# Two heads' attention scores on the two row halves of TensorE, in a two-layer adaLN transformer kernel

## The reference

```
qkv = x @ Wqkv
q = qkv[..., :512]    -> 32 query heads of 16      k, v -> 8 heads of 16
k = repeat(k, 4)                                    v = repeat(v, 2)
scores = q @ k^T / sqrt(16), causal over 2048 keys
aw = softmax(scores)
aw = aw[:, :, 0] - lam * aw[:, :, 1]                (pairs of heads)
attn = (aw @ v) * (1 - LAMBDA_INIT)
y = attn @ Wproj, then transposed, reshaped and @ Wproj again
```

## Time and profile before

| | |
|---|---|
| median of 3 runs | 2494.93 us (2493.49 to 2496.83) |
| span of the profiled execution | 2499.5 us |
| layer 0 attention, first to last pass | about 122 to 2013 us of the span |
| PE / DVE / ACT / POOL busy | 90% / 73% / 64% / 21% |
| granted TensorE clock, mean | 0.941 |

### The profile page before, as it was taken

How to read it: one execution, slowest core, us unless ns; L and a number is a source line. 1 busy time by engine, 2 the same in 40 slices (tenths; PEclk the granted TensorE clock), 3 DMA queues, 4 the chain that set the end, 5 groups by cost and what they waited for, 6 DMA issues and landing times. The chain is left out here.

```text
span 2499.5 us, 46449 instructions
## 1 busy us (share of the span) xinstructions
PE 2245.5 (90%) x13164; PEld 950.5 (38%) x13164; DVE 1826.9 (73%) x4038; ACT 1595.2 (64%) x3105; POOL 517.9 (21%) x573
## 2 busy tenths in 40 slices
PE   6799989999999999989998999899999869889984
PEld 4133323332333333333333333333333248657841
DVE  3888877877787787878787888788888528534467
ACT  2177767776777677767776767677777735335633
POOL 1113021221212121212121212121301014200067
PEclk8599999999999999999999999999999979899955
DMA  5210211112020202020202020202010030000001
GB/s 151 39 28 20 45 30 35 36 28 40 25 40 25 40 25 39 29 36 28 58 6 59 6 58 7 58 8 56 14 22 1 1 94 0 0 1 1 1 17 50
DMA packets 92964, 78.79 MB, mean 32 GB/s; under 512 B 47008, under 2 KB 79904, under 8 KB 92704
## 3 DMA queue, kind: packets, MB, share of 16 engines
q1 hardware_dynamic: 92704, 75.61, 13.3%
HBM read 26.81 MB, written 16.78 MB: 17 GB/s over the span
## 5 line engine op out<-in xcount | busy, mean ns | idle before, releaser
L726 ACT ACTIVATE probs<-b_bank 128x512 f32<-128x512 f32 (+1 forms) x2304 | 1224.1, 575 | 466.6 <-PE b_bank L883 438.1
L583 DVE TENSOR_REDUCE m_part<-a_bank 128x2 f32<-128x1024 f32 x768 | 917.2, 1221 | 202.7 <-PE a_bank L874 200.4
L883 PE MATMUL b_bank<-q_pack,k_pack 98*128 98x512 bf16 (+3 forms) x2560 | 798.9, 356 | 53.4 <-issue 26.0
L874 PE MATMUL a_bank<-k_pack,q_pack 96*128 96x512 bf16 (+3 forms) x2560 | 688.0, 358 | 67.5 <-DVE m_part L579 31.5
L901 PE MATMUL acc<-probs,v_tile 128*32 128x512 f32 (+3 forms) x5120 | 588.7, 541 | 14.6 <-ACT o_sb L733 14.1
L579 DVE CUSTOM_DVE_ANT_0 a_bank<-a_bank,mask_a 128x128 f32<-128x128 f32 (+3 forms) x1024 | 478.1, 518 | 145.2 <-PE a_bank L874 137.0
L883 PEld LDWEIGHTS b_bank<-q_pack,k_pack 98*128 98x128 bf16 x2560 | 240.2, 98 | 679.3 <-ACT probs L726 338.3
L449 POOL TENSOR_SCALAR_AFFINE_SELECT probs<-probs 128x512 f32<-128x512 f32 (+1 forms) x192 | 151.5, 789 | 1090.9 <-ACT probs L726 1090.9
L874 PEld LDWEIGHTS a_bank<-k_pack,q_pack 96*128 96x128 bf16 x2560 | 222.2, 99 | 314.8 <-DVE m_part L583 91.8
L901 PEld LDWEIGHTS acc<-probs,v_tile 128*32 128x32 f32 x5120 | 107.4, 108 | 242.6 <-issue 116.7
L579 DVE DVE_READ_ACCUMULATOR2_ANT m_part<- 128x1 f32 x1024 | 145.3, 142 | 0.1
(11 more groups left out here) (188 smaller groups left out, 1709.5 us busy)
## 6 DMA issues: line engine op xcount, KB each, us to landing
q_pack<-part SPq DMA_DIRECT2D x384, 64.0 KB, 2.4
scratch<-qkv_row SPq DMA_DIRECT2D x16, 512.0 KB, 2.8
heads<-scratch SPq DMA_DIRECT2D x16, 512.0 KB, 3.6
k_pack<-part SPq DMA_DIRECT2D x96, 64.0 KB, 2.3
xg<-in_L_attn_x SPq DMA_DIRECT2D x16, 256.0 KB, 2.8
scratch<-qkv_row SPq DMA_DIRECT2D x32, 128.0 KB, 2.7
q_pack<-m_rows SPq DMA_DIRECT2D x256, 2.0 KB
x<-in_L_attn_x SPq DMA_DIRECT2D x4, 1024.0 KB, 12.0
```

Of the source, the lines that this page charges most:

```text
L583: dve.tensor_reduce(m_part[:, 2 * hp:2 * hp + 2, t, c], bank[:, :, 0:w], AX.X, ALU.max).then_inc(a_maxed, A_INC)
L726: act.activation(probs[:, s % P_RING, h, at:C], b_bank[bank_no(("B", par, s, h))][:, at:C], ACT.Exp, scale=HD ** -0.5) \
L874: ins = pe.matmul(a_bank[unit % A_RING][:, k, 0:w], q_pack[buf][0:KP_ROWS, 2 * hp + k, q:q + P], k_pack[buf][0:KP_ROWS, C * c:C * c + w], ...
L883: ins = pe.matmul(b_bank[bank_no(("B", par, s, h))][:, at:at + C - q], k_pack[par][0:KP_ALL, P * kt:P * (kt + 1)], q_pack[par][0:KP_ALL, h ...
```

## The change

- q and k parts are packed again, in two slices of at most 64 rows: the first slice holds four pieces (64 rows), the second two pieces and the two maxima rows (34 rows). Even heads sit in partitions 0 to 63, odd heads in 64 to 127, and `k_pack` is there twice. A score tile of a step is now two accumulating matmuls (64 and 34 rows) on one row half of the array. A maxima tile is one matmul, of the first slice only.
- The stream of a step alternates between the halves (`two_heads`): head 0 first slice, the odd head's maxima tile, head 0 second slice, head 1 first slice, the even head's maxima tile, head 1 second slice. The matmuls that follow each other on different halves have different banks.
- The mask of a diagonal maxima tile is added by TensorE: two matmuls of 128 columns with 64 rows each (`pick` times `future`). DVE then does a plain reduction for each head and each tile.
- The rings are 3 single banks for the maxima, released head by head, and 4 for the steps.
- `pack` issues 36 DMAs in place of 30 (`k_pack` twice). POOL's constants grow from 13 to 24 instructions.
- The four hardware loops over passes are written out as straight code.

```diff
-PARTS_Q = (0, 0, 1, 1, 0, 2)
-PARTS_K = (0, 1, 0, 1, 2, 0)
+PARTS_Q = ((0, 0, 1, 1), (0, 2))
+PARTS_K = ((0, 1, 0, 1), (2, 0))
-A_RING = 2
-B_RING = 3
+SIDES = (1, 0)
+A_RING = 3
+B_RING = 4
...
-        a_bank = [ps(f"a_bank{i}", [P, 2, C]) for i in range(A_RING)]
+        a_bank = [ps(f"a_bank{i}", [P, C]) for i in range(A_RING)]
...
-                    for r, (pq, pk) in enumerate(zip(PARTS_Q, PARTS_K)):
-                        if pk == p:
-                            sp.dma_start(k_pack[buf][HD * r:HD * (r + 1), :], part[p][HD * QH:HD * (QH + 1), :]).then_inc(packs_in, 16)
+                    for n2 in range(2):
+                        for r, (pq, pk) in enumerate(zip(PARTS_Q[n2], PARTS_K[n2])):
+                            for side in range(2 if pk == p else 0):
+                                at = HALF * side + HD * r
+                                sp.dma_start(k_pack[buf][at:at + HD, n2, :], part[p][HD * QH:HD * (QH + 1), :]).then_inc(packs_in, 16)
...
+            made(pool.memset(pick[:, :, :], 0.0))
+            made(pool.memset(future[:, :, :], 0.0))
+            split_select(pick[:, 0, :], ALU.not_equal, 1.0, 0)
...
             for buf in range(2):
-                made(pool.memset(k_pack[buf][KP_ROWS:P, :], 1.0))
+                for side in range(2):
+                    at = HALF * side + SMALL
+                    made(pool.memset(k_pack[buf][at:at + 2, 1, :], 1.0))
...
-                if c == j:
-                    for k in range(2):
-                        dve.tensor_tensor_reduce(out=bank[:, k, 0:w], in0=bank[:, k, 0:w], in1=mask_a[:, C - w:C], scale=1.0,
-                                                 scalar=NEG, op0=ALU.add, op1=ALU.max,
-                                                 accum_out=m_part[:, 2 * hp + k, t, c:c + 1]).then_inc(a_maxed, A_INC // 2)
-                else:
-                    dve.tensor_reduce(m_part[:, 2 * hp:2 * hp + 2, t, c], bank[:, :, 0:w], AX.X, ALU.max).then_inc(a_maxed, A_INC)
+                for n, side in enumerate(SIDES):
+                    at = 2 * a_count(i, par, u) + n
+                    dve.wait_ge(a_scored, at + 1)
+                    dve.tensor_reduce(m_part[:, 2 * hp + side, t, c:c + 1], a_bank[at % A_RING][:, 0:width_a(u % UNITS)],
+                                      AX.X, ALU.max).then_inc(a_maxed, 1)
...
-            with dve.Fori(0, GROUPS // 2 - 1) as i:
-                body(Turns(i), False)
+            for i in range(GROUPS // 2 - 1):
+                body(i, False)
...
+            def unit_head(i, par, u, n):
+                rows = slice(HALF * side, HALF * (side + 1))
+                if at >= A_RING:
+                    pe.wait_ge(a_maxed, at - A_RING + 1)
+                ins = pe.matmul(a_bank[at % A_RING][:, 0:w], q_pack[buf][rows, hp, 0, q:q + P], k_pack[buf][rows, 0, C * c:C * c + w],
+                                start=True, stop=c < j)
...
+            def mask_head(i, par, u, n):
+                if c == j:
+                    for m in range(2):
+                        ins = pe.matmul(a_bank[at % A_RING][:, w - P:w], pick[rows, m, :], future[rows, m, :], start=False, stop=m == 1)
...
+            def two_heads(i, par, s, hp, ahead, last):
+                u = ahead[0] if ahead else None
+                score(i, par, s, 2 * hp, 0, last)
+                if u is not None:
+                    unit_head(i, par, u, 0)
+                score(i, par, s, 2 * hp, 1, last)
+                if u is not None:
+                    mask_head(i, par, u, 0)
+                score(i, par, s, 2 * hp + 1, 0, last)
+                if u is not None:
+                    unit_head(i, par, u, 1)
+                score(i, par, s, 2 * hp + 1, 1, last)
+                if u is not None:
+                    mask_head(i, par, u, 1)
+                for more in ahead[1:]:
+                    score_maxima(i, par, more)
```

More of the change, by code:

```diff
@@ L471, in body @@
                             split(2 * i + par + 2)
-            with pool.Fori(0, GROUPS // 2 - 1) as i:
-                body(Turns(i), False)
+            for i in range(GROUPS // 2 - 1):
+                body(i, False)
             body(GROUPS // 2 - 1, True)
@@ L757, in body @@
                                 first_part(g + 2)
-            with act.Fori(0, GROUPS // 2 - 1) as i:
-                body(Turns(i), False)
+            for i in range(GROUPS // 2 - 1):
+                body(i, False)
             body(GROUPS // 2 - 1, True)
@@ new lines, in mask_head @@
+            def mask_head(i, par, u, n):
+                j, t, c, hp = A_UNITS[u % UNITS]
+                side, w, at = SIDES[n], width_a(u % UNITS), 2 * a_count(i, par, u) + n
+                rows = slice(HALF * side, HALF * (side + 1))
+                if c == j:
+                    for m in range(2):
+                        ins = pe.matmul(a_bank[at % A_RING][:, w - P:w], pick[rows, m, :], future[rows, m, :], start=False, stop=m == 1)
+                    ins.then_inc(a_scored, 1)
+            def score_maxima(i, par, u):
+                for n in range(2):
+                    unit_head(i, par, u, n)
+                    mask_head(i, par, u, n)
@@ new lines, in score @@
+            def score(i, par, s, h, n2, last):
+                j, pieces = B_STEPS[s]
+                slot, top = ("B", par, s, h), (HALF, SMALL_ALL)[n2]
+                rows = slice(HALF * (h % 2), HALF * (h % 2) + top)
+                if n2 == 0:
+                    wait_for_bank(i, slot, last)
+                for n, (kt, at, q) in enumerate(pieces):
+                    ins = pe.matmul(b_bank[bank_no(slot)][:, at:at + C - q], k_pack[par][rows, n2, P * kt:P * (kt + 1)],
+                                    q_pack[par][rows, h // 2, n2, C * j + q:C * (j + 1)], start=n == n2 == 0, stop=n2 == 1,
+                                    skip_group_check=True)
+                if n2 == 1:
+                    ins.then_inc(b_scored, 1)
@@ L960, in _ @@
             pe.wait_ge(m_copied, len(NEXT))
-            with pe.Fori(0, GROUPS // 2 - 1) as i:
-                body(Turns(i), False)
+            for i in range(GROUPS // 2 - 1):
+                body(i, False)
             body(GROUPS // 2 - 1, True)
```

92 lines of the change are left out of this document (46 added, 46 removed).

## The result

The changed kernel takes 2431.2 us (2430.3 to 2432.32, 4 runs) against 2495.46 us for the kernel before, run beside it: a ratio of 0.974, 95% interval 0.973 to 0.976. It is faster by 64 us. The forecast was 2364, a gain of 131. The direction held and so did the overlap of the two halves, but half of the gain did not come. The time lies in the range of 2285 to 2450.

The account below looks back on a forecast made before the run. PE, its stream full, was taken as the bound. From 2499.5 us, 34 for joints and 105 for 15 passes of 8.2 − 1.2 came off, 8 for the start went on: 2368.5, less 4.6 gives 2364; 8-in-10 range 2285 to 2450.

Parts of the forecast that it names:

- Straight code: Loops over passes: writing them out removes six joints, 34 us in all (bounds 26 and 34), at no cost of its own.
- Scores on halves: PE's score and maxima matmuls: row halves overlap fully, so their streaming falls from 58.8 to 50.6 us a pass, 8.2 less.
- (b): Rival on PE's row halves: they do not overlap, 36.2 us more a pass, 3044 us in all; chance 0.09.
- (c): Rival on PE's weight loads: a half cannot load while it streams, 21 us more a pass, 2680 us; chance 0.04.
- DVE's own work: DVE's reductions: masks moved off DVE pay for the halved reductions, so it stays at 95.9 us busy a pass.
- Waits: Steps with three units load DVE more than PE; three buffered heads carry most; 1.2 us a pass charged, bounds 0 and 5.
- Rival (d): DVE and the ring of three take the gain: 0.2 us wait in each step, 7 us a pass, 2470 us; chance 0.08.
- Rival (a): The forecast itself: halves overlap, PE remains the bound, 3 to 12 us a pass gained, 2290 to 2425 us; chance 0.74.
- Fourth step bank: Four banks in place of three for the steps, worth the wait behind ACT, at most 1 or 2 us; nothing taken.
- SP and the maxima rows: SP's pack DMAs: maxima rows land at 29 us of the pass, just before step 10 at 29.6; further gains there lost.
- Start: Before the first maxima tile: POOL's memsets and small instructions cost 4.5 us, six more DMAs 3.7; +8 us, bounds 0 and +9.
- Last pass: Units only up to step 17; 38 blocks without a unit lose 8 us, about what the first half wins; 0 taken.

Follow-up runs that it names:

- experiment 2: Changed kernel, but DVE reduces only the first half of each maxima tile, so the maxima miss the other columns; 2324.59 us, one run.
- Experiment 6: Changed kernel, same units in each step, at most one per block of two heads, a third behind the product with v or the small job; 2413.1 us.
- experiment 10: Changed kernel with DVE's statistics, centring and gather cut into single instructions, one after each unit's reductions in certain steps; 2425.45 us.
- experiment 11: Changed kernel with the edits of Experiment 6 and experiment 10 together, and the first inverse deviation ahead of the four k_pack memsets; 2394.78 us.
- experiment 9: Changed kernel with four banks for maxima and three for steps, and DVE reducing only the first half of each maxima tile; 2396.84 us, one run.
- experiment 8: Changed kernel with both slices of a head one after the other on one half, then the maxima tile on the other; 2468.39 us, one run.

## Why the prediction came out as it did

**The bound.** Right as a reading of the step shown, and wrongly carried over. "PE's stream is full" held as long as DVE had slack. How much of the 117.6 us was waiting for DVE already is not known, since no run shortened the reductions of the kernel before. After the change DVE is busy for 96.1 of 114.9 us, 84%, and a tuned PE stream meets it in many steps.

**Straight code.** 34 us forecast, 37 measured. Right. By the two profiled executions the joints gave 33.6 and every one of the thirteen passes 0.6 more, 42 us up to the last pass; the profiled execution of before lay above its median, so that the medians show 37. Where the 0.6 us come from was not looked into.

**Scores on halves.** Right, and the largest unknown of the prediction, taken from one row of column tiles. Full overlap shows in the equal starts, and 109.4 us a pass was within 1 us of what experiment 2 measured. Rivals (b) and (c) are excluded by the same rows. The Trainium skill, "TensorE: Matmul & The Clock Gate", Part 3, has tiles start about 4 ns apart; the trace agrees, with starts that are equal to 0.01 us.

**DVE's own work.** Right: 96.1 us busy a pass against 95.9 forecast. By form, in the pass from 1049.4:

```profile
L605 DVE TENSOR_REDUCE m_part<-a_bank 128x1 f32<-128x512 f32 x113 | 71.2, 683 | 8.7 <-PE a_bank L894 6.3 <-PE a_bank L906 1.9
```

**Waits: the step that failed.** The prediction charged 1.2 us a pass, "bounds 0 and 5". It measured 6.2, outside its own bounds, and 5.0 us over 15 passes are 75 us, more than the 67 by which the time was missed. The reasoning counted six steps whose load on DVE is above PE's and let "three buffered heads (1.8 us) carry most". Two things are wrong in that. The three heads are not full at the start of a heavy step: a plain step already uses 4 × 0.60 = 2.40 us of DVE in 2.39 us of PE, as the prediction's own numbers give it, so there is no slack in which DVE could get ahead. And the side jobs of DVE (2.0, 1.1, 0.85 us and the outputs) were in its sum for the pass and not in any step. I read the first in the 2 us of the plain steps and the second in most of the 4 us of eight distances. Experiment 6 supports it by moving the tiles (1.1 of the 6.2 us), and experiment 10 shows that moving only the jobs is not enough. How the last 4 us a pass, which experiment 11 still loses against experiment 2, divide between the two was not measured. Nearly half of them stand in two distances, 4.16 against 3.23 behind the weighing of an output and 3.15 against 2.13 at the statistics. Rival (d) named this mechanism, with 0.2 us in each step and 7 us a pass, and gave it 0.08. The measured 6.2 us lies nearer to its number than to the forecast's, though the loss is not evenly spread. Rival (a), to which the forecast belongs and which had 0.74, fails by its own terms: 2.7 us a pass were gained where it had 3 to 12, and 2431 us lies above its bound of 2425. That the wider range holds the time is owed to the half of (d) that was added to it.

**Fourth step bank.** Nothing was taken; it is worth 4.3 us a pass (experiment 9). This did not spoil the sum, since a stream without ACT's waits was forecast (that was luck and not reasoning, as the bank was priced at "at most 1 or 2 us"), but it would have misled a choice between rings of 3 and 4 and of 4 and 3.

**SP and the maxima rows.** Held. In the pass from 1049.4 the issues stand here, and step 10 did not wait:

```profile
1072.54 0.58 SPq L365 DMA_DIRECT2D v_tile<-scratch  x1
1073.16 2.90 SPq L372 DMA_DIRECT2D q_pack<-m_rows  x4
```

PE's scores waited 1.8 us for these rows in the whole run. Step 10 started at 1081.10, 31.7 us into the pass and not 29.6; 1.7 of the difference are waits for DVE in the steps before it. That the next microsecond gained would be lost here did not come true: in experiment 2 the first ten steps are 1.7 us shorter, and no wait for the rows stands in its pass.

**Start.** +8 forecast; +8.65 at the first maxima tile, made as forecast of the late first rstd and the longer pack. Rows of after, POOL, SP and PE:

```profile
6.12 7.78 POOL L444 MEMSET k_pack<- 2x2048 bf16 x4
...
14.08 0.71 POOL L453 TENSOR_TENSOR rstd<-veps,expo 128x2 f32<-128x2 f32 x1
```
```profile
71.25 0.58 SPq L365 DMA_DIRECT2D v_tile<-scratch  x1
```
```profile
73.00 0.30 PE L894 MATMUL a_bank<-k_pack,q_pack 64*128 64x128 bf16 x2 [8.79 <-DMA q_pack<-part]
```

By the end of the first pass 3 us of it are won back, which leaves 5.5.

**Last pass.** 0 forecast, 3.5 us gained (99.4 to 95.9). Its 38 blocks of only two heads and its first half were only set against each other, and no run parts them.

In sum, in profiled time: 2368.5 us were forecast and 2428.4 measured, 60 too few. Fourteen passes hold 61 of it (thirteen gained 2.7 us and not 7.0, one of them 1.0 less, the next to last 2.9), each as the 5.0 us of the waits less some 0.7 by which the stream was better than costed. The first pass with the start holds 4.5 (+1 was forecast for its end, +5.5 measured); the last pass and the end of the kernel gave 3.4 and 2.2 back. The other 7 of the 67 are the profiled executions against their medians.

## What to carry to other kernels

When a change makes one engine's stream shorter, the next engine's slack must be read step by step, side jobs included, and not from its share of a pass: two engines at 96% and 84% of a pass that hand over through three banks lose 6 us of 115 to each other. Before changing how much work stands where, try the moment at which it is asked for; placing the same tiles singly was worth 18 us, and 36 with the consumer's side jobs cut up and an earlier start as well, while a plausible redistribution cost 57 us and a coarser exchange over the same banks 114, lower clock included. And a ring variant that measures "same" may hold two large opposite effects; halving the consumer's work separated them in one run.

## What the runs showed of the hardware that was not expected

A memset on GpSimd held up VectorE here, by as much as it lasts. In the last kernel the first rstd stands at 7.83 us in place of 14.08, and the four memsets of `k_pack` come behind it, from 8.59 to 16.02. VectorE's centring now runs beside them. Its timeline in experiment 11, and then in the changed kernel, where the memsets are over:

```profile
8.57 1.97 DVE L537 TENSOR_SCALAR xhat<-xg,mv,rstd 128x256 f32<-128x256 f32 x1 [0.83 <-POOL rstd L410]
10.46 1.97 DVE L538 TENSOR_SCALAR xhat<-xg,mv,rstd 128x256 f32<-128x256 f32 x1
```
```profile
14.82 0.41 DVE L536 TENSOR_SCALAR xhat<-xg,mv,rstd 128x256 f32<-128x256 f32 x1 [7.09 <-POOL rstd L453]
15.15 0.41 DVE L537 TENSOR_SCALAR xhat<-xg,mv,rstd 128x256 f32<-128x256 f32 x1
```

0.41 us became 1.97, and one memset lasts 1.86 (7.43 over four). Each centring seems to wait for the memset in front of it; so 3.1 us of the 6.25 won were lost at once. The Trainium skill, "SBUF — State Buffer", section "SBUF: two separate sides", says that the two engines share a pair of ports under a lock held for a whole instruction; the trace agrees, in that the slow-down is one memset. The next 0.7 went where a copy of DVE, `cmod`, took 1.63 us beside the memsets and 0.27 without them.

The rest went at the projection, and it went to TensorE's clock. The second group of four matmuls of 512 columns took 3.78 us where the changed kernel shows 1.98:

```profile
22.48 3.78 PE L853 MATMUL b_bank<-wqkv,hT 128*128 128x512 f32 x4 [0.47 <-ACT qkv_row L741]
```
```profile
23.86 1.98 PE L816 MATMUL b_bank<-wqkv,hT 128*128 128x512 f32 x4 [0.47 <-ACT qkv_row L704]
```

A window of the profile prints a granted clock of 1.00 for both stretches, but that is an empty record and no reading. The record begins at 17.3 us in the kernel before, at 21.3 in the changed kernel, at 26.2 in experiment 10 and at 26.8 in experiment 11, each time with the full level. In all four, the matmuls of 512 columns start 0.853 us apart before that moment and 0.429 after it. The same factor stands where the record does show both levels (PE busy, clock, DMA; changed kernel):

```profile
42.00:55.00 13.00, 11.82 (x48) 0.50 0.44 96
56.00:69.00 13.00, 8.21 (x39) 1.00 0.60 105
```

Products of 256 columns start 0.427 us apart in the first of these stretches and 0.216 in the second. So the start ran at the lower level up to the first record. In experiment 11 the work came sooner and the full level 5.5 us later; two groups of the projection ran at half speed for 0.95 and 1.80 us more, and the fourth group starts at 26.95 against 26.53. The first maxima tile stands at 72.95 against 73.00 us, so nothing of the earlier rstd arrived there. Experiment 10 starts like the changed kernel, with the same rstd at 14.08, and its clock rises 4.9 us later; its first maxima tile stands at 74.70. The late rise thus needs no earlier rstd; what sets its moment was not tried, and there is one profiled execution of each.

A memset's time on GpSimd went by its columns, not by its rows: two rows of 2048 took 1.80 us in three of four (2.23 in the first), as 32 rows did with 1.80 and 1.83.

By experiment 8, a matmul on a free half starts ahead of the one before it in the program that waits for the busy half, 0.22 us ahead in the step shown, and seems to be reported only in the program's order.
